# Grouped attention of one fused kernel: four key-value groups in phases, and the same work as eight overlapping half-steps

## Chip, cores and metric

The kernel runs on one NeuronCore of a Trainium2 chip, as one launch. The metric is the device time of that launch in microseconds (us), lower is better; it is the median of several executions. TensorE (PE in the profile, its weight loads PEld), VectorE (DVE), ScalarE (ACT), GpSimd (POOL) and SyncE (SP, which here only issues transfers) run their own instruction queues and meet at semaphores.

## What is computed

The program is eight blocks in a row (linear attention, mixture of experts, banded attention, LoRA experts, grouped attention, quantised feed-forward, selective scan, top-4 experts) on an activation `x` of 4 x 256 tokens by 256 channels. Before each block, `x` passes a gate: `sigmoid(x)` times a factor from a bidirectional decayed scan over a side input. The change touches the third and the fifth block.

- The fifth, grouped attention, has 16 query heads of width 128 in 4 groups; each group shares one key head and one value head. Per head: `q = rope(norm(x Wq))`, `k = rope(norm(x Wk))`, where the norm takes off the mean, divides by the root of the variance and applies a weight and a bias; then `softmax(q k^T / sqrt(128) + causal)` over 256 tokens of one batch entry, times `v`, times a gate `(1 + tanh(g/2))/2`, then `Wo`, added to `x`.
- The third, banded attention, has 16 heads of width 16 that see windows of 16-token blocks and 16 global tokens.

## The kernel before, in words

Everything is float32 with channels on the 128 partitions and the 1,024 tokens along the free axis, in two halves of 512 (`half(h)`, `HALF = 512`). PSUM is eight banks of 512 columns. A float32 matmul is two instructions on PE. All orders are written out by hand, one function for each engine; a signal such as `k["g_projected"]` counts, and `wait_ge(... .at(n))` waits until it was raised `n` times. An engine runs its queue in order, so what stands behind a wait waits too.

The grouped block (`grouped_*`) takes the 4 groups one after the other (`for g in range(m.KV)`), each in three phases over all 1,024 tokens:

1. Ten projections of 128x512 (key head and four query heads, two halves each; `JOBS`, L157), copied out by DVE (L1535), squared by ACT (L1603), summed over partitions by PE with `ones` (L157), `Ln` by ACT (L1610), then `Exp` on five blocks of 1,024 columns (L1613). Loads of ACT's function table (ACT_TABLE_LOAD) stand where `Ln` and `Exp` change places.
2. Gate and value projections with tanh (L1618) and copies (L1620), beside the rotation of the ten blocks: DVE scales and applies weight and bias (L1543, L1545), PE multiplies by a rotation matrix `g_rot`, POOL multiplies by the cosine (L1646), DVE by the sine and adds (L1551, L1553).
3. A loop over 16 units (a batch entry and a head): two score matmuls (L1703, L1704), masked maximum on DVE (L1577, L1580), exponential with row sums on ACT (L1633), reciprocal and normalisation on DVE (L1560, L1563), three transposes on PE (L1695), their copy by ACT (L1628), the product with `v` (L1713 to L1715), and the gate (L1570). Then the output projection `g_wo` for all tokens (L157) and the sum into `x` (L1590).

Beside this, `step(background, 1)` puts single instructions of the scans for blocks seven and eight (`wkv_vector`, `wkv_scalar`; L176 to L238) into the queues of DVE and ACT. In the banded block a loop over 16 groups of windows does masked scores (L1212, L1215), softmax on DVE and ACT (L1051 to L1062, L1114), transposes (L1203), their copy (L1110) and the product with values (L1231); DVE spreads the projected queries into block form (`banded_blocks`, L1012) straight from PSUM, and bank 3 is lent in turn to projections of queries and keys for later groups.

## Time and profile before

| | us |
|---|---|
| median of 3 runs | 2183.93 (2183.38 to 2186.18) |
| the profiled execution | 2181.16 |
| its span | 2179.9 |
| grouped block, from its first transfer to its last sum into `x` | 926.0 to 1443.3 |
| loop over groups in the banded block | 474.4 to 609.9 |

The profile is of one execution: its time is 2.8 us below the median of the runs, and its span 1.3 us below its time. The span is the time from the first to the last record. The busy share of an engine is an average over eight blocks with different limits, so the grouped and the banded block are read by themselves. "PEclk" is the granted TensorE clock as a share of full speed: 1.00 is 2.4 GHz and 0.50 is 1.2 GHz.

### The profile page before, as it was taken

Reading aid. Unit: us, or ns where it says so; the run is one execution under the profiler, and the core shown is the slowest. Engines: PE = TensorE matmul, PEld = TensorE weight load, DVE = VectorE, ACT = ScalarE, POOL = GpSimd, SP = SyncE. Lnnn points to the kernel's source line nnn. Section 1 sums busy time; section 2 is a strip of 40 time slices with the busy share of each in tenths; the row PEclk is TensorE's granted clock in tenths of the full one; section 3 lists DMA queues with packets and bytes.
Section 4 is the critical chain, followed back from the end, with each engine's and each line's share of the span. In section 5 each row is a group of like instructions: output and inputs, shape, how many; then the busy total and the mean of one; then the engine's idle time right before and its main releaser. Section 6 shows DMA issues by size and latency. Waiting matters only on the chain.

```text
span 2179.9 us, 17492 instructions
## 1 busy us (share of the span) xinstructions
PE 1703.0 (78%) x5814; PEld 948.5 (44%) x5814; DVE 1348.0 (62%) x2300; ACT 800.9 (37%) x1445; POOL 387.1 (18%) x261
## 2 busy tenths in 40 slices
PE   0699888877879999977887978764567777659999
PEld 0265444445643434335445453542222332226777
DVE  8474456454425636459486675876576898944565
ACT  4312434243322212243343453432354363313453
POOL 5000033110000101011020200100013765502332
PEclk9965899976759999998989989876577999969999
DMA  2000266150030000010000001000100000020110
GB/s 80 0 1 1 75 247 229 61 116 20 1 118 0 0 0 0 0 56 12 10 25 11 24 1 49 1 1 1 41 0 0 0 1 0 0 63 29 54 50 28
DMA packets 35839, 76.73 MB, mean 35 GB/s; under 512 B 5442, under 2 KB 22804, under 8 KB 33190
## 3 DMA queue, kind: packets, MB, share of 16 engines
q1 hardware_dynamic: 30662, 49.92, 7.3%
q0 software_dynamic: 5088, 25.69, 3.4%
q8 instruction: 47, 0.77, 0.2%
q14 instruction: 42, 0.34, 0.1%
HBM read 67.34 MB, written 7.21 MB: 34 GB/s over the span
## 4 chain that ended last, share of the span: by engine, by line
PE 56%; DVE 25%; issue 8%; ACT 6%; POOL 2%; PEldq 1%; DMA 1%; PEld 0%; SPq 0%; POOLq 0%; DVEq 0%; ACTq 0%
PE bank L157 41%; PE bank L2254 2%; PE bank L532 2%; PE bank L546 2%; PE bank L1215 2%; DVE g_q L1553 2%; PEldq L145 1%; DVE s_bu L2066 1%; POOL s_bu L2170 1%; DVE s_bu L2058 1%; DVE g_p L1577 1%; PE bank L1442 1%; DVE g_rs L1551 1%; DVE g_q L1543 1%; DVE g_p L1563 1%
## 5 line engine op out<-in xcount | busy, mean ns | idle before, releaser
L2170 POOL TENSOR_TENSOR s_bu<-s_rep,s_du 128x1024 f32<-128x1024 f32 x64 | 151.4, 2369 | 355.6 <-DVE s_du L2050 242.2
L2058 DVE TENSOR_TENSOR_SCAN s_bu<-bank,s_bu 128x1024 f32<-128x1024 f32 x64 | 145.8, 2279 | 22.9 <-ACT bank L2132 12.2
L2254 PE MATMUL bank<-s_bu,ident 128*128 128x512 f32 x256 | 133.6, 649 | 1.0 <-DVE s_dl L2007 0.3
L157 PE MATMUL bank<-e_xs,e_wsp 128*128 128x512 f32 x528 | 128.1, 391 | 0.0
L1646 POOL TENSOR_TENSOR g_q<-g_rs,g_rc 128x512 f32<-128x512 f32 x40 | 52.2, 1305 | 426.7 <-DVE g_rs L1545 426.7
L2132 ACT ACTIVATE bank<-s_dl,s_an 128x510 f32<-128x510 f32 x128 | 83.0, 682 | 106.1 <-DVE s_bu L2058 106.0
L157 PE MATMUL bank<-r_am,r_b 128*128 128x512 f32 x240 | 109.7, 597 | 0.0
L157 PEld LDWEIGHTS bank<-e_xs,e_wsp 128*128 128x128 f32 x528 | 99.1, 188 | 21.8 <-ACT e_cf L2444 0.7
L157 PE MATMUL bank<-conditioned,g_wqk 128*128 128x512 f32 x160 | 84.0, 656 | 21.6 <-DVE g_wqk L1530 21.6
L1406 POOL TENSOR_TENSOR r_ys<-r_y,r_y 128x512 f32<-128x512 f32 x14 | 22.8, 1631 | 433.7 <-DVE r_y L1351 433.7
L1633 ACT ACTIVATE g_p<-g_p,g_st 128x128 f32<-128x128 f32 (+1 forms) x128 | 57.2, 447 | 97.3 <-DVE g_st L1580 97.3
L2399 DVE TENSOR_TENSOR e_s<-e_s,bank 128x512 f32<-128x512 f32 (+1 forms) x50 | 34.3, 687 | 86.1 <-ACT e_s L2461 86.1
L2190 PE MATMUL bank<-s_bc,s_pick 96*128 96x512 bf16 x128 | 41.8, 411 | 56.4 <-DVE s_bu L2066 55.0
L2066 DVE TENSOR_TENSOR s_bu<-s_bu,bank 128x1024 f32<-128x1024 f32 x64 | 76.5, 1195 | 4.2 <-PE bank L2190 4.2
L157 PE MATMUL bank<-e_h,e_wdsp 128*128 128x512 f32 x264 | 75.6, 422 | 0.8 <-DVE e_h L2394 0.8
L157 PE MATMUL bank<-m_wgu,m_xs 128*128 128x512 f32 x120 | 61.9, 664 | 16.9 <-issue 15.5
L2254 PEld LDWEIGHTS bank<-s_bu,ident 128*128 128x128 f32 x256 | 52.5, 207 | 49.1 <-issue 40.9
L2461 ACT ACTIVATE e_s<-bank 128x512 f32<-128x512 f32 (+1 forms) x50 | 30.0, 599 | 116.1 <-PE bank L157 116.1
L157 PEld LDWEIGHTS bank<-r_am,r_b 128*128 128x128 f32 x240 | 46.3, 193 | 59.0 <-issue 59.0
L1603 ACT ACTIVATE g_sq<-g_q 128x512 f32<-128x512 f32 x40 | 25.2, 629 | 126.7 <-DVE g_q L1535 126.7
L1346 DVE TENSOR_TENSOR r_sl<-r_sl,bank 128x512 f32<-128x512 f32 x28 | 19.0, 678 | 82.8 <-ACT r_sl L1393 82.8
L1393 ACT ACTIVATE r_sl<-bank 128x512 f32<-128x512 f32 x28 | 16.7, 597 | 137.2 <-PE bank L157 134.1
(458 smaller groups left out, 3981.1 us busy)
## 6 DMA issues: line engine op xcount, KB each, us to landing
e_wgu<-in_e_gu SPq DMA_DIRECT2D x22, 256.0 KB, 2.7
b_vw<-b_values SPq DMA_DIRECT2D x48, 64.0 KB, 3.1
e_wd<-in_e_down SPq DMA_DIRECT2D x22, 128.0 KB, 2.6
r_w<-in_r_w SPq DMA_DIRECT2D x3, 896.0 KB, 7.9
...
```

What stands on the lines that cost most here:

```text
L157: last = e.matmul(out, lhs, rhs, start=start and n == 0, stop=stop and n == len(pairs) - 1, skip_group_check=True)
L532: last = e.matmul(banks[2 * (n % m.NPR) + i][:, cols], m.k4[j:j + 16, t, keys], m.q4[j:j + 16, t, b * T + part * P:(b + 1) * T], start=par ...
L546: last = e.matmul(bank[j:j + 32, cols], m.v[:, 2 * b + part, 32 * h:32 * h + 32], m.sm[2 * (o % m.NPR) + i][:, src], start=part == 0, stop ...
L1215: last = e.matmul(banks[n % 2][:, tile(at, m.KEYS)], m.qb[hh][:, 8 * g + w, :], m.kw[hh][:, 8 * g + w, :], start=False, stop=True, skip_gr ...
L1553: e.tensor_tensor(o, o, r, ALU.add).then_inc(k["g_q_ready"].up(), 1)
L1633: e.activation(s[:, cols], s[:, cols], ACT.Exp, bias=m.st[:, 0, c + i:c + i + 1], scale=m.SC, accum_out=m.st[:, 1, c + i:c + i + 1]).then_ ...
L1646: e.tensor_tensor(both(o), both(r), table(m.rc), ALU.mult).then_inc(k["g_cos"].up(), 1)
L2058: e.tensor_tensor_scan(b, flat(k.pairs[n % 2][:, :, :]), b, 0.0, ALU.mult, ALU.add).then_inc(k["s_scanned"].up(), 1)
L2066: e.tensor_tensor(b, b, flat(k.pairs[2][:, :, :]), ALU.mult).then_inc(k["s_weighted"].up(), 1)
L2132: e.activation(banks[2 * (n % 2) + i][:, :].rearrange("p (b t) -> p b t", t=T)[:, :, 1:T], m.dl[:, et, half(h)].rearrange("p (b t) -> p b ...
L2170: e.tensor_tensor(m.bu[n % m.NBU][:, :, :], m.rep[:, 2 * np:2 * np + 2, :], m.du[:, et, half(h)].unsqueeze(1).to_broadcast([P, 2, HALF]), ...
L2254: summed = e.matmul(banks[6][:, :], k.ident[:, :], m.bu[(n - 1) % m.NBU][:, i, :], start=np == 0 and i == 0, stop=np == m.NP - 1 and i == ...
```

## The change

In the grouped block the unit of work becomes a step `f`: one group on one half of the tokens, eight steps in all (`STEPS`). Ten passes run over eight slots each (`UNITS`); in a pass, `new` projects step n, `now` does scores and softmax for step n-1, and `old` finishes step n-2. Five projections share banks 0 and 1 with four gate projections (`grouped_free`), the sums have bank 2, scores banks 3 and 4, transposes bank 5, mixing bank 6; bank 7 holds first the values and then the two output projections. The transposes of four heads go into one bank and are copied and mixed at once (48 matmuls of 512 columns for 64 times three of 128). The rotation matrix goes: POOL multiplies by the cosine and, for half of the partitions, by the sine; DVE does the other half and the sum. Weight and bias move from DVE to ACT (`grouped_affine`); ACT first copies each variance out of the bank and takes `Ln` and `Exp` in two calls for each step. Grouped buffers now lie over those of the next block's weights, whose transfers move to the end of the block. The scans take two background steps in each slot of the first six passes. In the banded block, ACT copies the queries of the later groups to SBUF and POOL spreads them (12 of 16 calls); the projections into bank 3 move to earlier turns.

```diff
-def banded_blocks(k, e, n, bank):
+def banded_blocks(k, e, n, queries, done):
...
     own = m.heads[:, :].unsqueeze(1).unsqueeze(3).to_broadcast([P, 8, 8, m.Q])
-    e.wait_ge(*k["b_q"].at(n // 4 + 1))
-    e.tensor_tensor(m.qb[hh][:, 8 * g:8 * g + 8, :].rearrange("p w (h q) -> p w h q", q=m.Q), src, own, ALU.mult).then_inc(k["b_blocks"].up(), 1)
+    e.tensor_tensor(m.qb[hh][:, 8 * g:8 * g + 8, :].rearrange("p w (h q) -> p w h q", q=m.Q), src, own, ALU.mult).then_inc(done.up(), 1)
 
 
...
-        for at, first, bank in ((0, 4, 6), (4, 8, 3), (8, 12, 3)):
-            if at <= n < at + 2:
-                for i in range(2):
-                    banded_blocks(k, e, first + 2 * (n - at) + i, banks[bank])
...
+def banded_queries(k, e, n, bank):
+
+    m = k.banded
+    e.wait_ge(*k["b_q"].at(n + 1))
+    if n > 1:
+        e.wait_ge(*k["b_blocks"].at(4 * n - 4))
+    e.copy(m.qs[:, :], bank[:, :]).then_inc(k["b_queries"].up(), 1)
 
...
             banded_keys(k, e, 1, banks[7])
...
+        if n in (2, 6):
+            banded_queries(k, e, 2 + n // 6, banks[3])
+        if n in (4, 8):
+            banded_keys(k, e, 2 + n // 8, banks[3])
 
...
 
 
 def banded_tensor(k, e):
...
-        if n == 3:
+        if n == 2:
             project(1, 0, m.wq, banks[3], k["b_q"])
+        if n == 4:
+            e.wait_ge(*k["b_queries"].at(2))
+            project(1, 0, m.wk, banks[3], k["b_k"])
         if n == 6:
-            e.wait_ge(*k["b_blocks"].at(12))
-            project(1, 0, m.wk, banks[3], k["b_k"])
-        if n == 7:
             e.wait_ge(*k["b_keys"].at(9))
             project(1, 1, m.wq, banks[3], k["b_q"])
-        if n == 10:
-            e.wait_ge(*k["b_blocks"].at(16))
+        if n == 8:
+            e.wait_ge(*k["b_queries"].at(3))
             project(1, 1, m.wk, banks[3], k["b_k"])
...
-    NP = 5
-    JOBS = [(hd, h) for hd in [4, 0, 1, 2, 3] for h in range(NH)]
-    UNITS = [(b, hd) for b in range(NB) for hd in range(4)]
+    STEPS = 4 * NH
...
+def grouped_pieces(m, n):
...
+def grouped_rope(k, e, f, j):
+    m, n = k.grouped, 5 * f + j
+    turn, o = m.turn[n % 2], m.q[f % 2][:, j, :]
+    e.wait_ge(*k["g_affine"].at(n + 1))
+    e.tensor_tensor(both(turn[0:64, :]), both(m.rs[64:P, j, :]), table(m.rsn[64:P, :]), ALU.mult).then_inc(k.v_steps.sem, 1)
+    e.wait_ge(k.v_steps.sem, k.v_tick())
+    e.wait_ge(*k["g_cos"].at(n + 1))
+    e.wait_ge(*k["g_sin"].at(n + 1))
+    e.tensor_tensor(o, o, turn[:, :], ALU.add).then_inc(k["g_roped"].up(), 1)
...
+def grouped_gate(k, e, a, b, t):
+    m = k.grouped
+    th = m.th[a % 2][:, :, b * T + t * P:b * T + (t + 1) * P]
+    e.wait_ge(*k["g_mixed"].at(6 * a + 3 * b + (3 if t else 1)))
+    e.wait_ge(*k["g_tanh"].at(4 * a + 4))
+    e.scalar_tensor_tensor(th, th, 1.0, k.banks[6][:, :].rearrange("p (h q) -> p h q", h=m.R), ALU.add, ALU.mult).then_inc(k["g_gated"].up(), 1)
...
+    for n in range(m.PASSES):
+        new, now, old = grouped_pieces(m, n)
+        for s in range(m.UNITS):
+            if now is not None:
+                grouped_greatest(k, e, now, s)
+            if s and now is not None:
+                grouped_normal(k, e, now, s - 1)
+            if s == 0 and old is not None:
+                grouped_normal(k, e, old, m.UNITS - 1)
+                grouped_gate(k, e, old, 0, 1)
+            if now is not None and s in (0, 1, 2):
+                grouped_rope(k, e, now, 2 + s)
+            if now is not None and s == 0:
+                grouped_scale(k, e, now, 4)
+            if s in (2, 4) and old is not None:
+                grouped_gate(k, e, old, 1, s // 2 - 1)
+            if s == 6 and now is not None:
+                grouped_gate(k, e, now, 0, 0)
+            if s in (6, 7) and old is not None:
+                if n == m.PASSES - 1 and s == 6:
+                    run_out(background)
+                    arrive(k, e)
+                grouped_add(k, e, old, s - 6)
+            if new is not None:
+                if s < 5:
+                    grouped_copy(k, e, new, s)
+                if s == 5:
+                    grouped_scale(k, e, new, 0)
+                    grouped_scale(k, e, new, 1)
+                if s == 6:
+                    grouped_scale(k, e, new, 2)
+                    grouped_rope(k, e, new, 0)
+                if s == 7:
+                    grouped_rope(k, e, new, 1)
+                    grouped_scale(k, e, new, 3)
+                    if n % 2 and n // 2 + 1 < m.KV:
+                        grouped_centre(k, e, n // 2 + 1)
+                step(background, 2)
+
+
...
+def grouped_root(k, e, f, first, last):
+    m = k.grouped
+    rs = m.rs[:, first:last, :]
+    e.wait_ge(*k["g_variance"].at(5 * f + last))
+    e.activation(rs, rs, ACT.Ln).then_inc(k.a_steps.sem, 1)
+    e.wait_ge(k.a_steps.sem, k.a_tick())
+    e.activation(rs, rs, ACT.Exp, scale=-0.5).then_inc(k["g_root"].up(), 1)
...
+def grouped_tanh(k, e, f, i):
+    m = k.grouped
+    e.wait_ge(*k["g_gate"].at(4 * f + i + 1))
+    if f >= 2:
+        e.wait_ge(*k["g_down"].at(2 * f - 2))
+    e.activation(m.th[f % 2][:, i, :], k.banks[(9 * f + 5 + i) % 2][:, :], ACT.Tanh, scale=0.5).then_inc(k["g_tanh"].up(), 1)
...
+def grouped_values(k, e, f):
+    m = k.grouped
+    e.wait_ge(*k["g_value"].at(f + 1))
+    if f >= 2:
+        e.wait_ge(*k["g_mixed"].at(6 * f - 6))
+    e.copy(m.v[f % 2][:, :], k.banks[7][:, :]).then_inc(k["g_values_out"].up(), 1)
...
+    for n in range(m.PASSES):
+        new, now, old = grouped_pieces(m, n)
+        for s in range(m.UNITS):
+            turn = grouped_turn(s, new, now, old)
+            if turn is not None:
+                grouped_turned_out(k, e, *turn)
+            if new is not None and s == 7:
+                grouped_tanh(k, e, new, 0)
+            if now is not None:
+                grouped_exp(k, e, now, s)
+            if now is not None and s == 0:
+                grouped_tanh(k, e, now, 2)
+                grouped_affine(k, e, now, 4)
+                grouped_tanh(k, e, now, 3)
+            if new is not None:
+                if 1 <= s <= 5:
+                    grouped_square(k, e, new, s - 1)
+                if 2 <= s <= 6:
+                    grouped_variance(k, e, new, s - 2)
+                if s == 4:
+                    grouped_root(k, e, new, 0, 3)
+                if s == 5:
+                    grouped_values(k, e, new)
+                    grouped_affine(k, e, new, 0)
+                    grouped_affine(k, e, new, 1)
+                if s == 6:
+                    grouped_affine(k, e, new, 2)
+                    grouped_root(k, e, new, 3, 5)
+                if s == 7:
+                    grouped_tanh(k, e, new, 1)
+                    grouped_affine(k, e, new, 3)
+                step(background, 2)
     run_out(background)
+
...
+    e.wait_ge(*k["load_g"].at(48))
+    for f in range(m.STEPS):
+        for j in range(m.R + 1):
+            n, r = 5 * f + j, m.rs[:, j, :]
+            e.wait_ge(*k["g_affine"].at(n + 1))
+            if n:
+                e.wait_ge(*k["g_sin"].at(n))
+            e.tensor_tensor(both(m.q[f % 2][:, j, :]), both(r), table(m.rc[:, :]), ALU.mult).then_inc(k["g_cos"].up(), 1)
+            if n >= 2:
+                e.wait_ge(*k["g_roped"].at(n - 1))
...
+def grouped_free(k, e, f, i):
...
+def grouped_output(k, e, l, c):
+    m = k.grouped
+    e.wait_ge(*k["g_gated"].at(4 * l + 4))
+    e.wait_ge(*k["load_g_wo"].at(16 * (l // 2 + 1)))
+    if c:
+        e.wait_ge(*k["g_added"].at(2 * l + 1))
+    else:
+        e.wait_ge(*k["g_values_out"].at(min(l + 3, m.STEPS)))
+        if l:
+            e.wait_ge(*k["g_added"].at(2 * l))
+    mm(e, k.banks[7][:, :], [(m.wo[:, hd, tile(c)], m.th[l % 2][:, hd, :]) for hd in range(m.R)]).then_inc(k["g_down"].up(), 1)
...
+    for n in range(m.PASSES):
+        new, now, old = grouped_pieces(m, n)
+        for s in range(m.UNITS):
+            turn = grouped_turn(s, new, now, old)
+            if now is not None:
+                grouped_scores(k, e, now, s)
+            if turn is not None:
+                grouped_transpose(k, e, *turn)
+            if new is not None:
+                if s < 5:
+                    grouped_project(k, e, new, s)
+                if s == 4:
+                    grouped_project_values(k, e, new)
+            if s in (5, 6) and old is not None:
+                grouped_output(k, e, old, s - 5)
+            if new is not None and s > 5:
+                grouped_project_gate(k, e, new, 2 * s - 12)
+                grouped_project_gate(k, e, new, 2 * s - 11)
+            if turn is not None:
+                grouped_mix(k, e, *turn)
+            if new is not None and 1 <= s <= 5:
+                grouped_sums(k, e, new, s - 1)
```

The order of the queues, at three places. First PE in the middle of the grouped block. Names: `ident` with `g_p` are transposes, `g_pt` with `g_v` is the mixing, `g_th` with `g_wo` the output projection. Before, the end of a loop and what follows it:

```order
L1715 MATMUL bank<-g_pt_216,g_v 128x128
L1713 MATMUL bank<-g_pt_217,g_v 128x128
L1714 MATMUL bank<-g_pt_217,g_v 128x128
L1715 MATMUL bank<-g_pt_217,g_v 128x128
L157 MATMUL bank<-g_th,g_wo 128x512 x16
L157 MATMUL bank<-conditioned,g_wqk 128x512 x4
```

Now, the end of slot 4 and slot 5 of a pass:

```order
L157 MATMUL bank<-conditioned,g_wqk 128x512 x2
L157 MATMUL bank<-g_wgv,conditioned 128x128 x8
L157 MATMUL bank<-g_sq_200,ones 128x512
L1852 MATMUL bank<-g_q_209 128x128
L1853 MATMUL bank<-g_q_209 128x256
L1862 MATMUL bank<-ident,g_p_216 128x128
L1862 MATMUL bank<-ident,g_p_217 128x128
L1862 MATMUL bank<-ident,g_p_218 128x128
L1862 MATMUL bank<-ident,g_p_219 128x128
L157 MATMUL bank<-g_th_210,g_wo 128x512 x4
L1872 MATMUL bank<-g_pt_224,g_v_213 128x512
L157 MATMUL bank<-g_sq_199,ones 128x512
```

The output projection, 16 matmuls in one piece before, is now two pieces of 4 in each pass, and the first stands behind the values' projection, whose bank it takes over.

Second ACT at the same place, slots 4 and 5 (L1697 is `Ln`, L1699 `Exp`, L1739 the copy of the values, L1723 the copy of the transposes):

```order
L1697 ACT_TABLE_LOAD
L1697 ACTIVATE g_rs<-g_rs 128x1536
L1699 ACT_TABLE_LOAD
L1699 ACTIVATE g_rs<-g_rs 128x1536
L1723 COPY g_pt_224<-bank 128x512
L1714 ACTIVATE g_p_221,g_st<-g_p_221,g_st 128x128
L1714 ACTIVATE g_p_221,g_st<-g_p_221,g_st 128x256
L1682 ACTIVATE g_sq_200<-g_q_209 128x512
L1690 ACTIVATE g_rs<-bank,eps 128x512
L1739 COPY g_v_213<-bank 128x512
L1706 ACTIVATE g_rs<-g_rs,vecs 128x512 x2
```

The two table loads, once for each group before, now come twice in each step, and the copy of the values stands behind them. In the whole program ACT has 24 table loads more.

Third PE in the banded loop, turns 2 to 4. Before, and then now:

```order
L1203 MATMUL bank<-ident,b_s_155 128x128 x4
L1212 MATMUL bank<-b_msk,b_hot 128x512
L1215 MATMUL bank<-b_kw_151,b_qb_149 128x64 x8
L1231 MATMUL bank<-b_pt_159,b_vw 128x128 x8
L157 MATMUL bank<-b_xn,b_wq 128x512 x2
L1203 MATMUL bank<-ident,b_s_156 128x128 x4
```

```order
L157 MATMUL bank<-b_xn,b_wq 128x512 x2
L1217 MATMUL bank<-ident,b_s_155 128x128 x4
L1226 MATMUL bank<-b_msk,b_hot 128x512
L1229 MATMUL bank<-b_kw_151,b_qb_149 128x64 x8
L1245 MATMUL bank<-b_pt_159,b_vw 128x128 x8
L1217 MATMUL bank<-ident,b_s_156 128x128 x4
```

The projection of the queries for groups 8 to 11 went one turn up, ahead of the first transposes.

## Rows read from the trace of the kernel before

**Rows 1.** The page: busy time of the engines, share of the span, instructions

```profile
PE 1703.0 (78%) x5814; PEld 948.5 (44%) x5814; DVE 1348.0 (62%) x2300; ACT 800.9 (37%) x1445; POOL 387.1 (18%) x261
```

**Rows 2.** Windows: the grouped block (length, busy PE, PEld, DVE, ACT, POOL, clock, DMA)

```profile
925.00:1445.00 520.00, 422.72 (x1539) 248.34 (x1537) 355.26 (x905) 216.85 (x517) 52.20 (x40) 0.90 0.06 20
```

**Rows 3.** Groups by line in 925 to 1440 (busy, mean ns, idle before, releaser)

```profile
L157 PE MATMUL bank<-g_rs,g_rot 128*128 128x512 f32 x80 | 45.1, 648 | 20.9 <-DVE g_rs L1545 20.9
L1545 DVE TENSOR_SCALAR g_rs<-g_q,vecs 128x512 f32<-128x512 f32 x40 | 25.2, 629 | 1.5
L201 DVE TENSOR_TENSOR wkv_db<-wkv_db,wkv_euk 128x1024 f32<-128x1024 f32 x4 | 4.9, 1224 | 0.0
```

**Rows 4.** Timeline, phase 1 of the first group (start, us, instruction)

```profile
952.72 1.88 PE L157 MATMUL bank<-conditioned,g_wqk 128*128 128x512 f32 x4
954.43 1.02 PE L157 MATMUL bank<-g_sq,ones 128*128 128x512 f32 x2
954.63 0.69 DVE L1535 COPY g_q<-bank 128x512 f32<-128x512 f32 x1 [1.29 <-PE bank L157]
955.24 0.68 DVE L186 TENSOR_TENSOR_SCAN wkv_nb<-decay,ekv 128x256 f32<-128x256 f32 x1
955.29 1.88 PE L157 MATMUL bank<-conditioned,g_wqk 128*128 128x512 f32 x4
955.36 0.63 ACT L1603 ACTIVATE g_sq<-g_q 128x512 f32<-128x512 f32 x1 [1.37 <-DVE g_q L1535]
955.89 0.67 ACT L1610 ACTIVATE g_rs<-bank,eps 128x512 f32<-128x512 f32 x1
```

**Rows 5.** Timeline, one unit of the softmax loop

```profile
1419.59 0.28 DVE L1577 CUSTOM_DVE_ANT_0 g_p<-bank,g_msk 128x128 f32<-128x128 f32 x1
...
1420.21 0.39 PE L1703 MATMUL bank<-g_q 128*128 128x128 f32 x2
...
1420.34 0.16 DVE L1560 RECIPROCAL g_st<-g_st 128x2 f32<-128x2 f32 x1
...
1420.46 0.40 ACT L1633 ACTIVATE g_p<-g_p,g_st 128x128 f32<-128x128 f32 x1 [0.39 <-DVE g_st L1580]
...
1420.87 0.38 PE L1713 MATMUL bank<-g_pt,g_v 128*128 128x128 f32 x2
...
1420.99 0.41 DVE L1570 SCALAR_TENSOR_TENSOR g_th<-g_th,bank 128x256 f32<-128x256 f32 x1
...
1421.36 0.46 ACT L1628 COPY g_pt<-bank 128x384 f32<-128x384 f32 x1
```

**Rows 6.** Timeline, ACT from the last `Ln` to the five `Exp` of 1,024 columns

```profile
964.93 0.69 ACT L1610 ACTIVATE g_rs<-bank,eps 128x512 f32<-128x512 f32 x1 [0.64 <-PE bank L157]
965.63 1.28 ACT L1613 ACT_TABLE_LOAD   x1
966.93 4.84 ACT L1613 ACTIVATE g_rs<-g_rs 128x1024 f32<-128x1024 f32 x5
```

**Rows 7.** Timeline, POOL and DVE in the rotation

```profile
974.47 1.27 POOL L1646 TENSOR_TENSOR g_q<-g_rs,g_rc 128x512 f32<-128x512 f32 x1 [1.81 <-DVE g_rs L1545]
975.03 1.26 DVE L1553 TENSOR_TENSOR g_q<-g_q,g_rs 128x512 f32<-128x512 f32 x1
```

**Rows 8.** Windows, as rows 2, around the block's first matmuls

```profile
939.00:940.00 1.00, 1.00 (x2) 0.34 (x1) 0.44 (x1) 0.00 (x0) 0.00 (x0) 0.50 0.00 0
940.00:942.00 2.00, 2.00 (x6) 0.87 (x5) 1.15 (x3) 1.64 (x2) 0.00 (x0) 0.91 0.00 0
```

**Rows 9.** Timeline, PE's first matmul behind the end of a background job

```profile
1039.61 0.80 PE L1713 MATMUL bank<-g_pt,g_v 128*128 128x128 f32 x2 [4.26 <-ACT g_pt L1628]
```

**Rows 10.** Waits in 455 to 626, the banded block (total us, times, longest)

```profile
PE bank L157 <- DVE b_qb L1012: 6.6, 2, 3.3
...
PE bank L157 <- ACT b_kw L1085: 4.0, 1, 4.0
```

**Rows 11.** The page: its costliest group (busy, mean ns, idle before, releaser)

```profile
L2170 POOL TENSOR_TENSOR s_bu<-s_rep,s_du 128x1024 f32<-128x1024 f32 x64 | 151.4, 2369 | 355.6 <-DVE s_du L2050 242.2
```

401 lines of the change are left out of this document (184 added, 217 removed).

## Prediction

> **What bounds the kernel now.** I read the page first: PE is busy for 78% of the span and DVE for 62% [rows 1], so neither alone sets the time. Then the windows of the block that changes most: the grouped block takes 926.0 to 1443.3, 517.3 us, with PE busy for 423 of 520 us and DVE for 355 [rows 2]. PE's records overlap and many ran at half clock, so I count PE by its distances instead. Last I read the timeline for the distance from one instruction to the next and from one engine to the next, because the new order is a ring of waits and only such distances price it.
>
> The distances, at full clock. A projection holds PE for 1.71 us (952.72 to 954.43) and one product of 512 columns for 0.86 (954.43 to 955.29). DVE starts 1.91 after a projection starts, so 0.20 after its end; ACT's square starts 0.73 later; a 512-column op holds DVE for 0.61, and a square holds ACT for 0.53 [rows 4]. Two scores take 0.66 (1420.21 to 1420.87); by the same row a transpose is 0.11, four 0.44. Maximum and shift hold DVE for 0.75 (1419.59 to 1420.34), normalisation for 0.65 (to 1420.99). The exponential starts 0.87 after the maximum starts and holds ACT for 0.90 (1420.46 to 1421.36) [rows 5]. A table load is 1.28; 1,024 columns take 0.97 on ACT (4.84 for five), so 512 more cost about 0.43 and 1,536 columns 1.45 [rows 6].
>
> **Part 1, work removed and added in the grouped block.** The rotation matrix goes: 40 products of 0.86, 34 us of PE (its records sum to 45.1) [rows 3]. DVE loses 40 ops of 0.63, 25 us [rows 3]. ACT gains 40 affine calls of some 0.62, 25 us, and 24 table loads, 31 us. POOL goes from 40 ops of 1.27 to 80 [rows 7], for half of the partitions in the new ones; I give them the same 1.27, since the length is the same. In a steady pass PE then has 41 us (5 projections, 4 gates and the values at 1.71, 5 sums and 6 mixings at 0.86, 2 output pieces of 3.43, scores 5.3, transposes 2.6), DVE 42 and ACT 36. If nothing waited, eight passes would take some 340 us. They do wait.
>
> A rule of the Trainium skill bears on the loads. The trace shows one load ahead of the five `Exp` [rows 6] after one ahead of `Ln`, so two for each change there and back. The page "ScalarE: Activation LUTs" (Table sets: the hidden batching unit) says that one set holds both `ln` and `exp`, so that the pair needs one load. By it the sum below would be about 16 loads, 20 us, shorter. The queue as built has two, and I count two.
>
> **Part 2, one steady pass, slot by slot.** `G` is the start of DVE's maximum. The ring of slots 1 to 4 is: scores 0.66 and 0.20 to DVE, 0.87 and 0.90 for the exponential, square 0.53, variance 0.69, 0.05 to PE, sums 0.86. That is 4.8 us, where PE has 4.5 to 5.0 of work.
> - Slot 0: the first projection waits for a bank that ACT's third tanh frees, behind the exponential: 0.86 + 0.87 + 0.90 + 0.6 + 0.05 + 1.71 = 5.0.
> - Slot 1: DVE is last. Its slot 0 holds maximum, normalisation, gate, rotation (1.33), scale and copy, and two background steps (0.77 each on average: in the 24 steps of a job 16 scans of 0.6 [rows 4], some six ops of 1.2 [rows 3] and two shorter ones), 6.1 us. Behind them come two POOL ops. A DVE op with two SBUF inputs that starts while POOL multiplies ends 0.55 after it: 1.26 us instead of 0.68 [rows 7]. Two such waits add 2.5. So `G` is at 9.5, and the slot ends 3.3 later at 12.8: 7.8 us.
> - Slot 2: the mixing waits for the gate, behind DVE's rotation: 6.8. Slots 3 and 4: 4.8 and 4.9.
> - Slot 5: ACT issues the square root behind slot 4's variance: 0.70 + 1.30 + 1.48 + 1.30 + 1.50 = 6.3 us. Behind it stand the copy of the transposes, exponential, square, variance (0.5 + 0.9 + 0.5 + 0.6), then the copy of the values. PE's output projection needs the bank of the values. From the start of the variance, ACT has copied them after 6.3 + 2.5 + 0.6 = 9.4 us; PE begins slot 5 at 1.8, has 1.1 of scores and transposes, and then waits 6.5. Then come 3.43 + 0.86 + 0.86: 12.8.
> - Slot 6: scores and transposes 1.1; the second output piece waits 2.5 for DVE (maximum, normalisation, gate, add); then 3.43, two gates 3.42 and mixing 0.86: 11.3. Slot 7: the third gate waits for the first tanh, behind ACT's second square root (4.7): 6.8.
>
> The sum is 60.2 us, against 64.7 for half a group now (517.3 / 8).
>
> **Part 3, the block.** The first matmul comes at 8.1 instead of 9.8 us, the weights' transfer being first in SP's queue. Pass 0 has new work only: five turns of 1.71 + 0.86 and the values to ACT's variance at 14.3, then in a row square root 6.1, square to second affine 3.0, third affine 1.3, second root 4.7, tanh 0.6 and two gates 3.4: 33.5. Pass 1 has no `old`, so that slots 5 and 6 are 8.0 and 5.4, slot 7 with ACT behind it 8.7, and the centring 1.3: 52.5 with the first five slots at 29. Passes 2 to 5: 4 x 60.2, and 4 us twice for the centring of weights behind DVE's slot 7: 249. Passes 6 and 7 without background: 113. In pass 8, without projections, DVE's rotation and the two output pieces leave 33.5; pass 9 is three rounds of transposes, copy and mixing at 2.1, a gate, and two output pieces of 3.43 with their sums, 17. Each of four background jobs ends in two `Ln`/`Exp` calls of ACT with two loads; such an end cost PE 4.26 us before [rows 9] and stands in the ring again: 17. Together 8.1 + 515.5 = 524 us, +6 against 517.3.
>
> To this comes the clock. At the block's first matmuls, after 9.9 us without work, the granted share was 0.50 (1.2 GHz) up to 940 and then rose [rows 8]: four dense microseconds did two us of work. In rows 9 PE came back slow after 4.3 us without work too. Slot 5's gap of 6.5 us comes in six passes, slot 6's of 2.5 and slot 1's of 3 as well. I take 2 us for the first and 1 for each of the others, 4 x 6, and 11 for the thin first and last passes: 35 us. Its ends are 10 (only the long gaps) and 55 (each gap costs 2). The Trainium skill states the direction in "TensorE: Matmul & The Clock Gate" (Part 1): throttled is the default and activity releases it. Grouped block: +41.
>
> **Part 4, the banded block.** PE waits 6.6 us for DVE's spread queries and 4.0 for the copied keys [rows 10]; the earlier turns take both away, 10.6. The four projections also move under the normalisation that PE waits for anyway, about 1.8 us each, 7. Against it: 12 POOL ops of 2.37 or more [rows 11], during which DVE's one two-input op of each turn (L1062) waits up to 2.4; I take 5 in all. Together -13, with ends -22 (no contention, a warmer clock) and 0 (every turn held).
>
> **Small edits.** Mixing four heads at once has the same columns and fewer instructions: nothing, hidden in PE's gaps. `Ln` from SBUF after a separate variance copy is in the ring above. The later transfer of the next block's weights starts behind pass 7, some 50 us before its first reader: nothing; if that cover went, it would be one transfer of some 7 us.
>
> Sum: +41 - 13 = +28. The profiled execution would go from 2181.2 to 2209; the median stands 2.8 higher, so 2183.9 + 28 = **2212 us**.
>
> **The rivals.**
> - *PE does not wait for the values in slot 5* (faster). If ACT reached the copy as early as PE its bank, 6.5 us x 6 = 39 and the cold start behind it, 2 x 6 = 12, go: 2212 - 51 = 2161. It decides in that one wait of PE: the change gains once it is under some 3 us. For it: ACT is the least busy of the three, at 36 us in a pass, and my ring may stack waits that in truth overlap. Against it: ACT's queue order is fixed and the two loads are measured. 0.22.
> - *The clock stays up.* The gaps are mostly shorter than the 4.3 and 9.9 us that brought the low clock here, and my 35 us fall away: 2177, with 2168 to 2190 around it. 0.16, half of it faster, half the same.
> - *GpSimd and DVE collide on the path.* I charge 2.5 us in a pass. If each POOL op held DVE in full, 80 x 1.27 = 102 us, some 40 more would reach the ring: 2252. For it: scans, scale, rotation and sum all read two SBUF inputs. Against it: POOL works mostly in slots 5 to 7, where DVE has slack. 0.12.
> - That the change doesn't do what it says is excluded by the order of the queues.
>
> **How the numbers follow.** My case has 0.50, and spans 2190 to 2235 by its clock term. A measurement of this kernel can tell about 0.2%, 4.4 us, from no change. Faster: 0.22 + 0.08 = 0.30. The same: 0.08. Slower: 0.50 + 0.12 = 0.62. The range goes from 2150 (the first rival and the banded block at its better end) to 2250 (the collision's own value); some tenth lies outside on each side.
>
> **What would show it.** PE idle before the first output projection, released by ACT's L1739, 5 to 8 us in each of six passes; passes of 62 to 68 us; a granted clock in the block below the 0.90 of now; DVE's two-input ops lengthened beside POOL; no wait of PE for b_qb or b_kw. Passes under 60 us, or no wait of PE at L1739, make it wrong.

## The result and the profile after

The changed kernel takes **2208.12 us** (median of 4 runs, 2207.24 to 2209.95) against 2183.65 for the kernel before on the same chip: 1.0111 times, 95% interval 1.0093 to 1.0128. It is 24.5 us slower, and the prediction was 2212. Its profiled execution has a span of 2206.0 us. Two executions (3013.6 us of the kernel before, 2651.1 of the one with the roots without loads) ran at a granted clock of 0.62 to 0.63 and are left out of all times and intervals below.

The page of the changed kernel, the line that answers to [rows 1], and the two groups of matmuls of the grouped block in front of which PE waits most (busy us, mean ns, idle before and what ended it):

```profile
PE 1672.5 (76%) x5446; PEld 901.1 (41%) x5446; DVE 1326.0 (60%) x2216; ACT 875.4 (40%) x1484; POOL 471.5 (21%) x313
...
L157 PE MATMUL bank<-g_th,g_wo 128*128 128x512 f32 x128 | 77.3, 760 | 57.7 <-ACT g_v L1739 38.9
L157 PE MATMUL bank<-conditioned,g_wqk 128*128 128x512 f32 x160 | 86.7, 670 | 36.5 <-ACT g_th L1731 29.0
```

PE and DVE have less work than before, ACT and POOL more. What grew is PE's idle time, the number behind each bar. The waits of PE in 900 to 1500 (engine, what waits, what it waits for: total us, times, longest):

```profile
PE bank L157 <- ACT g_th L1731: 45.9, 15, 7.7
PE bank L157 <- ACT g_v L1739: 38.9, 6, 7.5
PE bank L157 <- DVE residual L1626: 18.0, 8, 2.4
```

Six waits of some 6.5 us for the copied values (6.2 to 7.5) and eight of up to 2.4 for the add of the first output piece stand there, the two that the prediction's slots 5 and 6 named. The 15 waits for a tanh (L1731) are those of its slots 0 and 7: 2.5 to 7.7 us in slot 0, 1.3 in slot 7 of passes 2 to 7. The window over the whole block, as in [rows 2]:

```profile
911.00:1488.00 577.00, 403.12 (x1197) 208.06 (x1196) 356.87 (x886) 294.14 (x572) 113.19 (x80) 0.87 0.05 18
```

The granted clock is 0.87 against 0.90. The block runs from its first transfer at 911.1 to the end of its last add at 1470.8, 559.7 us against 517.3: +42.4. The banded part in front of it became shorter: from the start of its loop to its output projections it took 135.5 us (474.4 to 609.9), now 123.0 (473.6 to 596.6), 12.5 less. That its loop also starts 0.8 us earlier need not be the change's: in the 13 traces of this case the loop starts at 470 to 481 us, behind work that no edit touches. So the length of a block tells more than its place. PE's waits in the banded part, in 470 to 640, no longer hold the two lines of [rows 10]; the longest in total is:

```profile
PE bank L1217 <- DVE b_s L1063: 17.9, 10, 2.4
```

Now the timeline of one steady pass of the grouped block, slots 5 and 6 (start us, us, instruction, idle before and its releaser):

```profile
1110.94 0.67 ACT L1690 ACTIVATE g_rs<-bank,eps 128x512 f32<-128x512 f32 x1
...
1111.63 1.28 ACT L1697 ACT_TABLE_LOAD   x1
...
1112.81 0.39 PE L1852 MATMUL bank<-g_q 128*128 128x128 f32 x2
1112.92 1.48 ACT L1697 ACTIVATE g_rs<-g_rs 128x1536 f32<-128x1536 f32 x1
...
1114.42 1.28 ACT L1699 ACT_TABLE_LOAD   x1
...
1115.72 1.48 ACT L1699 ACTIVATE g_rs<-g_rs 128x1536 f32<-128x1536 f32 x1
...
1119.55 0.57 ACT L1739 COPY g_v<-bank 128x512 f32<-128x512 f32 x1
...
1120.38 5.25 PE L157 MATMUL bank<-g_th,g_wo 128*128 128x512 f32 x8 [6.31 <-ACT g_v L1739]
...
1127.18 0.38 PE L1852 MATMUL bank<-g_q 128*128 128x128 f32 x2
...
1130.05 0.69 DVE L1626 SCALAR_TENSOR_TENSOR residual<-bank,residual 128x512 f32<-128x512 f32 x1
...
1130.88 3.67 PE L157 MATMUL bank<-g_th,g_wo 128*128 128x512 f32 x8 [2.45 <-DVE residual L1626]
```

From the start of ACT's variance to the end of the copied values it is 9.2 us (1110.94 to 1120.1); 9.4 was predicted. Both table loads of the root are there. PE starts slot 5 at 1112.81, is out of work after 1.3 us and waits 6.31. The first output piece then takes 5.25 us where the second, behind a shorter wait, takes 3.67. The granted clock (the number behind POOL's) says why: 0.69 in the first, 1.00 in the second.

```profile
1120.38:1125.46 5.08, 5.08 (x8) 2.24 (x9) 0.00 (x0) 1.17 (x2) 4.11 (x4) 0.69 0.00 0
1130.88:1134.39 3.51, 3.51 (x9) 1.60 (x10) 3.44 (x5) 3.00 (x3) 1.99 (x2) 1.00 0.00 0
```

The distance from one unit's scores (L1852) to the next gives the length of each slot. Measured, in us, for the seven passes that have both a `now` and a `new` step, passes 1 to 7 (pass 1 has no `old` one); the last row is the prediction's, without its clock term:

| pass | 0 | 1 | 2 | 3 | 4 | 5 | 6 | 7 | sum |
|---|---|---|---|---|---|---|---|---|---|
| 1 | 7.0 | 6.4 | 7.4 | 5.6 | 6.7 | 9.8 | 5.5 | 13.4 | 61.9 |
| 2 | 5.1 | 9.0 | 6.8 | 4.9 | 5.0 | 14.7 | 13.2 | 6.9 | 65.6 |
| 3 | 8.7 | 5.6 | 6.6 | 4.9 | 5.0 | 14.4 | 11.5 | 6.9 | 63.6 |
| 4 | 10.0 | 6.1 | 9.4 | 5.1 | 6.7 | 15.8 | 13.1 | 6.9 | 73.0 |
| 5 | 6.4 | 7.0 | 6.7 | 4.9 | 5.0 | 14.7 | 13.1 | 6.9 | 64.8 |
| 6 | 12.0 | 5.6 | 6.3 | 4.9 | 5.0 | 14.5 | 13.0 | 6.9 | 68.4 |
| 7 | 6.4 | 5.0 | 6.3 | 4.9 | 5.0 | 14.2 | 11.5 | 6.9 | 60.2 |
| predicted, steady | 5.0 | 7.8 | 6.8 | 4.8 | 4.9 | 12.8 | 11.3 | 6.8 | 60.2 |

### The profile page after: what moved, and what is told of

Its sections match the earlier page's. It is cut to its first block, busy times and chain, and to the rows that moved or that the text cites. A ratio compares the mean times of both kernels' runs of the same rounds, so it can differ in the third digit from the quotient of the medians.

```text
span 2206.0 us, 16987 instructions
## 1 busy us (share of the span) xinstructions
PE 1672.5 (76%) x5446; PEld 901.1 (41%) x5446; DVE 1326.0 (60%) x2216; ACT 875.4 (40%) x1484; POOL 471.5 (21%) x313
## 4 chain that ended last, share of the span: by engine, by line
PE 57%; DVE 20%; ACT 11%; issue 7%; POOL 2%; DMA 1%; PEldq 1%; PEld 0%; POOLq 0%; DVEq 0%; SPq 0%; ACTq 0%
PE bank L157 40%; PE bank L2445 2%; PE bank L532 2%; PE bank L546 2%; PE bank L1229 2%; POOL s_bu L2361 1%; PE bank L1872 1%; DVE s_bu L2257 1%; PE bank L1456 1%; DVE s_bu L2249 1%; ACT g_p L1714 1%; PEldq L145 1%; DVE g_p L1599 1%; PE bank L563 1%; PE bank L1853 1%
## 5 line engine op out<-in xcount | busy, mean ns | idle before, releaser
L1599 DVE CUSTOM_DVE_ANT_0 g_p<-bank,g_msk 128x128 f32<-128x128 f32 (+1 forms) x128 | 40.5, 354 | 149.3 <-PE bank L1853 149.2
L157 PE MATMUL bank<-g_th,g_wo 128*128 128x512 f32 x128 | 77.3, 760 | 57.7 <-ACT g_v L1739 38.9
L1723 ACT COPY g_pt<-bank 128x512 f32<-128x512 f32 x48 | 27.9, 582 | 147.1 <-PE bank L1862 147.0
L157 PE MATMUL bank<-conditioned,g_wgv 128*128 128x512 f32 x128 | 62.2, 631 | 16.9 <-ACT g_th L1731 16.9
L157 PE MATMUL bank<-m_wgu,m_xs 128*128 128x512 f32 x120 | 61.9, 664 | 16.9 <-issue 15.5
L2663 POOL TENSOR_TENSOR e_wsp<-e_wgu,e_wsp 128x512 fp32r<-128x512 f32 x22 | 33.4, 1520 | 182.8 <-ACT e_wsp L2609 182.8
```

Of the source, the lines that this page charges most:

```text
L157: last = e.matmul(out, lhs, rhs, start=start and n == 0, stop=stop and n == len(pairs) - 1, skip_group_check=True)
L1599: e.tensor_tensor_reduce(s[:, cols], k.banks[3 + n % 2][:, cols], m.msk[:, cols], 1.0, -BIG, ALU.add, ALU.max, m.st[:, 0, c + i:c + i + 1] ...
```

## The experiments

All times below are medians; "to before" is the distance to the kernel before in the same series (2182.3, 2181.2 or 2181.8 us), which for the changed kernel was +24.5. The interval is that of the ratio to the kernel before. The difference of two such distances is uncertain by some 5 to 8 us, as their two intervals together say. "Block" is the length of the grouped block in the one trace of each kernel, from its first transfer to its last add; it was 517.3 before and 559.7 in the changed kernel. It leaves out what varies ahead of the block, and so is the finer measure of an edit there, but of one execution.

| kernel | us | to before | ratio, 95% interval | block |
|---|---|---|---|---|
| banded part alone | 2171.0 | -11.3 | 0.9935 to 0.9967 | 517.4 |
| changed kernel, values first | 2203.7 | +21.3 | 1.0071 to 1.0116 | 552.8 |
| changed kernel, roots without loads | 2196.2 | +13.9 | 1.0043 to 1.0085 | 548.3 |
| changed kernel, POOL's products cut | 2193.8 | +11.5 | 1.0038 to 1.0103 | 545.7 |
| changed kernel, PE filled, 8 gaps | 2203.3 | +22.0 | 1.0070 to 1.0130 | 557.9 |
| changed kernel, PE filled, 6 gaps | 2195.0 | +13.2 | 1.0047 to 1.0091 | 545.9 |
| changed kernel, add first | 2181.6 | +0.4 | 0.9995 to 1.0026 | 534.6 |
| values first and add first | 2160.9 | -20.3 | 0.9880 to 0.9927 | 514.4 |
| and tanh first, steps dealt by slot | 2160.9 | -20.3 | 0.9884 to 0.9939 | 510.8 |
| values and add first, 12 steps a pass | 2151.1 | -30.7 | 0.9851 to 0.9881 | 503.7 |
| and tanh first | 2143.8 | -38.0 | 0.9813 to 0.9839 | 496.3 |

### The banded part alone

The kernel before, with the change's edits from the class `Banded` down to the banded part's tensor code and nothing of the grouped block.

> The kernel before with the banded part of the change alone. Theory (the turns placed earlier take PE's two waits for the spread queries and the copied keys away, 10.6 us, hide 7 of the projections and give back 5): -13, so about 2171 us, with ends at -22 and 0. Rival (the banded part gives nothing, since GpSimd's spreading is slower than DVE's, and the whole +24.5 comes from the grouped part): 2184 us.

Measured 2171.0, 11.3 below the kernel before, by the ratio 7 to 14 below. The theory holds and the rival falls; the grouped block is as long as before, 517.4 us. PE's waits in 470 to 640 show the same line, 17.9 us in ten waits, as in the changed kernel, and neither of the two.

So the slowdown of 24.5 is the sum of a gain of some 11 in the banded part and a loss in the grouped block, of about 36 us by these runs and of 42.4 by its length in the one trace.

### The values ahead of the first root

```diff
                 if s == 4:
+                    grouped_values(k, e, new)
                     grouped_root(k, e, new, 0, 3)
                 if s == 5:
-                    grouped_values(k, e, new)
```

> The changed kernel, ACT's copy of the values put ahead of the first square root instead of behind it. Theory (PE's 6.5 us before the first output piece hang on that copy alone; behind it the mixing and the sum wait for ACT's copy of the transposes and square, which still stand behind the root): PE's wait for L1739 goes, a shorter one comes before the mixing and the sum, so that 4.8 of the 6.5 us go in each of six passes, 29, and some 6 to 12 of cold restarts: about 2170 us. Rival (all of it goes, 6.5 x 6 = 39 and 12): 2157. Rival (the root's delay gives it back elsewhere in the ring): 2200 to 2208.

Measured 2203.7, and +21.3 instead of +24.5, which these runs cannot tell from no gain; the block is 6.9 us shorter. The first rival falls, and so does my forecast of 2170: this is the case in which the time is given back. The timeline of this kernel, the same pass:

```profile
1119.42 0.59 ACT L1739 COPY g_v<-bank 128x512 f32<-128x512 f32 x1 [0.53 <-PE bank L157]
...
1120.08 0.38 PE L1852 MATMUL bank<-g_q 128*128 128x128 f32 x2
...
1121.17 3.60 PE L157 MATMUL bank<-g_th,g_wo 128*128 128x512 f32 x8
...
1129.54 0.64 PE L1852 MATMUL bank<-g_q 128*128 128x128 f32 x2
```

Slot 5 is 9.5 us (1120.08 to 1129.54) instead of 14.4, as the theory said: 4.9 gained. But slot 6 is now 15.7 instead of 11.5. Over passes 2 to 7 slot 5 gives 31 us and slot 6 takes 21 of them back. Half of the 21 is the wait for the add (the change had 18.0, longest 2.4):

```profile
PE bank L157 <- DVE residual L1626: 28.4, 8, 4.2
```

The timeline of slot 6 shows what lengthened it. First the changed kernel, then this one:

```profile
1128.71 0.17 DVE L1602 TENSOR_SCALAR g_st<-g_st 128x2 f32<-128x2 f32 x1
...
1128.98 0.55 DVE L1612 TENSOR_SCALAR g_p<-g_p,g_st 128x128 f32<-128x128 f32 x2
```

```profile
1131.67 1.26 POOL L1790 TENSOR_TENSOR g_q<-g_rs,g_rc 128x512 f32<-128x512 f32 x1
1131.74 1.21 DVE L1602 TENSOR_SCALAR g_st<-g_st 128x2 f32<-128x2 f32 x1
...
1133.05 1.63 DVE L1612 TENSOR_SCALAR g_p<-g_p,g_st 128x128 f32<-128x128 f32 x2
1133.07 1.26 POOL L1794 TENSOR_TENSOR g_turn<-g_rs,g_rsn 64x512 f32<-64x512 f32 x1
...
1136.02 5.12 PE L157 MATMUL bank<-g_th,g_wo 128*128 128x512 f32 x8 [4.14 <-DVE residual L1626]
```

DVE adds the first output piece behind the maximum, shift and normalisation of slot 6. PE is now early, so that slot 6 falls beside POOL's products, which in the changed kernel were over before it: in all six passes the shift takes 0.9 to 1.2 us instead of 0.17 and the normalisation 1.6 instead of 0.55, and the add comes that much later. Behind the longer wait the second output piece is slow in all six passes (5.1 to 6.5 us, against four of six), and in four of six the scores ahead of it run at a granted 0.50. It is not ACT that DVE waits for in slot 6: the exponential that the normalisation needs ended 2.2 to 3.0 us before the slot began. The step that I had missed: the second output piece needs DVE, and how long DVE takes to the add depends on what POOL does at that time.

### The square roots without table loads

```diff
-    e.activation(rs, rs, ACT.Ln).then_inc(k.a_steps.sem, 1)
+    e.activation(rs, rs, ACT.Square).then_inc(k.a_steps.sem, 1)
```

> The changed kernel with the logarithm in the grouped block's square roots replaced by a square, which needs no table load; what is computed there is no longer the inverse root, every instruction keeps its size. 32 loads of 1.28 us go, 41 us of ACT. Theory (both roots of a pass stand in the ring, the first in front of the values in slot 5, the second in front of the tanh in slot 7): -2.6 in slot 5 and up to -2.6 in slot 7 in each of eight passes, -30 to -41, and a little of the clock, so 2165 to 2178 us. Rival (only the first root counts, the second is covered by PE's output piece and gates): 6 x 2.6 = 16 to 20, 2188 to 2192. Rival (ACT is not what the ring hangs on): above 2200.

Measured 2196.2, +13.9 instead of +24.5: 10.6 us for 32 loads of 1.28, that is 41 us of ACT. Nearest to the first rival, though under its 16 to 20. The trace is of an execution at 2206.6, 10 us above the median, but it is late ahead of the block already, which starts at 920.8 instead of 911.1; the block itself is 11.4 shorter. The wait of PE for the values fell by 2.6 each time, from 38.9 for six to:

```profile
PE bank L157 <- ACT g_v L1739: 23.6, 6, 4.9
```

Slot 7 stayed at 6.9 in passes 2 to 7, so there the second root's loads cost nothing. The third gate waits for a tanh that stands behind the copy of the transposes, and that copy waits for PE's transposes of the same slot, not for the root. The trace of the changed kernel agrees: the root is over 1.8 to 3.4 us before the slot begins, and ACT idles 3.0 to 4.7 us ahead of that copy:

```profile
1135.86 1.06 ACT L1699 ACTIVATE g_rs<-g_rs 128x1024 f32<-128x1024 f32 x1
...
1139.97 0.58 ACT L1723 COPY g_pt<-bank 128x512 f32<-128x512 f32 x1 [3.05 <-PE bank L1862]
```

My account of slot 7 had the right length for the wrong reason. Only in pass 1, whose slot 6 is short, does slot 7 hang on the root: it fell from 13.4 to 9.3. The slot lengths also tell where the rest went: slot 5 is 12.3 us shorter over passes 2 to 7 and pass 1 is 4.2 shorter; slots 0 and 1 of pass 2, behind DVE's centring of the next weights, are 2.9 longer (17.0 against 14.1), and slot 6, slow in five passes instead of four, 1.9.

### GpSimd's products cut to 8 columns

```diff
+            w = T if n < 2 else 4
-            e.tensor_tensor(both(m.q[f % 2][:, j, :]), both(r), table(m.rc[:, :]), ALU.mult)...
+            e.tensor_tensor(both(m.q[f % 2][:, j, :])[:, :, 0:w], both(r)[:, :, 0:w], table(m.rc[:, :])[:, :, 0:w], ALU.mult)...
```

and the same for the sine product: 76 of the 80 products of the block, not 78 as the text below has it, since both products of the first two heads stay whole.

> The changed kernel with GpSimd's products of the rotation (78 of its 80 ops in the grouped block) cut to 8 columns each; the rotation is then left incomplete. It prices all that GpSimd does to DVE and to the ring. Theory (two held DVE ops in a steady pass, 2.5 us, and the length of the products themselves in the rotation's chain hidden): -15 to -25, 2183 to 2193 us. Rival (GpSimd and DVE collide on the path in full): -40 or more, 2168 or less. Rival (DVE has slack everywhere): above 2203.

Measured 2193.8, +11.5 instead of +24.5: 13 us by the medians and 9 by the ratios, with runs from 2189.5 to 2203.1; the block is 14.0 shorter. That is just under the 15 to 25 of the theory; the full collision falls. The edit takes away both the holding of DVE and the length of the products themselves, and the run does not separate the two. The seven passes of the table sum to 444.8 instead of 457.5, 12.7 less, most of it (11.4) in slots 0 and 1. The groups of DVE, first of the changed kernel, then of this one (busy, mean ns, idle before):

```profile
L186 DVE TENSOR_TENSOR_SCAN wkv_db<-decay,ek 128x256 f32<-128x256 f32 x16 | 16.5, 1030 | 0.0
...
L1602 DVE TENSOR_SCALAR g_st<-g_st 128x2 f32<-128x2 f32 x64 | 14.3, 224 | 2.2
```

```profile
L186 DVE TENSOR_TENSOR_SCAN wkv_db<-decay,ek 128x256 f32<-128x256 f32 x16 | 11.9, 745 | 0.0
...
L1602 DVE TENSOR_SCALAR g_st<-g_st 128x2 f32<-128x2 f32 x64 | 10.9, 170 | 2.2
```

Without POOL's products beside it a scan is back from 1,030 ns to 745, and even the two-column shift from 224 to 170.

### PE filled while it waits for the values

```diff
+        for _ in range(6):
+            e.matmul(k.banks[6][:, :], k.ones[:, :], m.th[l % 2][:, 0, :], start=True, stop=True, skip_group_check=True)
         e.wait_ge(*k["g_values_out"].at(min(l + 3, m.STEPS)))
```

> The changed kernel with six products of 512 columns (5.2 us at full clock, written to a bank that the next mixing overwrites) put into PE's wait before each step's first output piece. Nothing else moves. In the changed kernel's trace the piece behind the 6.3 us wait takes 5.25 us, the same eight products at full clock 3.6. Theory (the gap without work brings the low clock, which lengthens the first piece by 1.65 in six passes and slot 6 by 1.6 in four): -10 to -16, so 2192 to 2198 us, and first pieces of 3.6. Rival (the low clock does not hang on this gap): 2208, pieces of 5.2 as before.

Measured 2203.3, +22.0, against a forecast of 2192 to 2198. Slot 5 came down from 14.5 to 12.6 us in five of six passes, as the theory wanted. But the edit puts the products into all eight steps, and in passes 8 and 9 PE has no such wait: the two last passes took 70 us instead of 59. The test was cut too wide, so it was made again with `range(6 if l < 6 else 0)`:

> As e5_warm, but the six extra products stand only ahead of the six first output pieces that had the 6.3 us wait, and not in passes 8 and 9, where PE had no such wait and e5_warm therefore paid 5.2 us twice. In e5_warm slot 5 came down from 14.5 to 12.6 us in these six passes. Theory (that is the whole price of this gap's low clock, 1.9 x 6 = 11): -11 to -13 against the changed kernel, 2195 to 2198 us. Rival (the clock's saving is given back elsewhere): 2203 as in e5_warm, or more.

Measured 2195.0, +13.2: 11.3 less than the change by the medians (9 by the ratios), the predicted 11 to 13; the block is 13.8 shorter. In the timeline the same eight products start behind a wait of 0.96 and are over 3.54 us later at a granted 1.00, where they took 5.08 (1120.38 to 1125.46) at 0.69 in the changed kernel:

```profile
1112.13 5.32 PE L1883 MATMUL bank<-g_th,ones 128*128 128x512 f32 x12
1118.41 3.70 PE L157 MATMUL bank<-g_th,g_wo 128*128 128x512 f32 x8 [0.96 <-ACT g_v L1739]
1121.95 1.02 PE L1872 MATMUL bank<-g_pt,g_v 128*128 128x512 f32 x2
```

No dependence changed and no useful work was added, so this is the price of the low clock behind the gap of slot 5. By the slots it is 1.9 us in each of five passes; in pass 4, where a wait of 2.0 was left behind the fill, the piece stayed slow (granted 0.68) and 0.4 was gained. Another 3 us came in slot 6, slow now in two passes instead of four. Together that is about a third of what the grouped block loses. The Trainium skill, "TensorE: Matmul & The Clock Gate" (Part 1), states the direction: the throttled clock is the default, and activity releases it. The trace agrees: 0.69 behind a wait of 6.31, 1.00 behind the fill.

### The add of the first output piece first in slot 6, alone and with the values first

```diff
         for s in range(m.UNITS):
+            if s == 6 and old is not None and n < m.PASSES - 1:
+                grouped_add(k, e, old, 0)
             if now is not None:
                 grouped_greatest(k, e, now, s)
```

> The changed kernel, DVE's add of the first output piece put first in slot 6, ahead of the maximum, the normalisation of unit 5 (which waits for an exponential behind the square root) and the gate; ACT's order as it is. Theory (PE's 2.4 us before the second output piece hang on that order): -2.4 in seven passes, 17, and some of the low clock in slot 6: 2186 to 2192 us. Rival (the mixing behind it waits instead): above 2203.

Measured 2181.6, +0.4 instead of +24.5: 24 us (22 by the ratios), at or above the upper end of the 16 to 22 that I expected. Slot 6 is 8.8 us in all six steady passes instead of 11.5 or 13.1: the 2.4 of the wait are gone, and so is the 1.6 of slow clock, which had come in four of the six. The 2.4 were DVE's own maximum, shift, normalisation and gate behind PE's scores, not a wait for ACT: in the changed kernel the exponential that the normalisation needs ended 8.4 to 9.0 us before slot 6. With this one line moved the changed kernel is level with the kernel before, though its grouped block is still longer (534.6 against 517.3): the banded part pays for the rest.

Both edits in one kernel:

> The changed kernel with both: the values copied ahead of the first root and the add first in slot 6. With the values alone, slot 5 fell from 14.5 to 9.5 us and slot 6 rose from 11.5 or 13.1 to 15.7, because PE then waited 4.2 instead of 2.4 for the add. Theory (the two waits hand the time to each other and only the two edits together free it): slot 5 at 9.5 and slot 6 at 9, a pass 9 us shorter, six times, -54: 2154 us (2145 to 2165). Rival (the two edits only add, -4.4 and -17): 2187. Rival (a third wait takes over, as the second did): above 2195.

Measured 2160.9, -20.3, that is some 45 below the changed kernel where the two edits alone gave 3 and 24 (by the blocks 45.3, where they gave 6.9 and 25.1). The rival that they only add (2187) falls: in passes 2 to 7 slot 5 is 9.0 to 10.3 and slot 6 8.8 to 10.1, and the grouped block, 514.4 us, is for the first time shorter than the 517.3 of the kernel before. The timeline of this kernel, slots 5 and 6:

```profile
1106.02 3.60 PE L157 MATMUL bank<-g_th,g_wo 128*128 128x512 f32 x8
...
1112.86 0.67 DVE L1626 SCALAR_TENSOR_TENSOR residual<-bank,residual 128x512 f32<-128x512 f32 x1
...
1115.06 3.60 PE L157 MATMUL bank<-g_th,g_wo 128*128 128x512 f32 x8
```

Both output pieces take 3.60 and neither waits. It is not the full 54: slot 7, 6.9 in passes 2 to 7 of every kernel so far, is now 7.3 to 9.8 in five of the six. The trace shows ACT's second root reaching into it. In pass 3, the copy of the transposes follows the root's `Exp` (L1701) without a pause, the tanh follows the copy, and PE waits for the tanh:

```profile
1124.32 1.06 ACT L1701 ACTIVATE g_rs<-g_rs 128x1024 f32<-128x1024 f32 x1
...
1125.28 0.57 ACT L1725 COPY g_pt<-bank 128x512 f32<-128x512 f32 x1
...
1125.74 0.60 ACT L1733 ACTIVATE g_th<-bank 128x512 f32<-128x512 f32 x1
...
1126.49 5.37 PE L157 MATMUL bank<-conditioned,g_wgv 128*128 128x512 f32 x8 [2.44 <-ACT g_th L1733]
```

It is so in exactly the five passes with the longer slot. In these POOL's products again hold slot 6's shift (0.7 to 1.1 us) and normalisation (1.6), and the root stands behind them. No run takes the root out of this kernel, so what it costs there is not measured.

### The background work dealt out otherwise

```diff
-                step(background, 2)
+                step(background, (1, 1, 1, 3, 3, 3, 2, 2)[s])
```

in DVE's and ACT's loops, and in ACT's `grouped_tanh(k, e, new, 0)` ahead of `grouped_turned_out` in slot 7.

> The kernel of e7_both, and also ACT's first tanh ahead of the copy of the transposes in slot 7, and the background steps dealt out as 1, 1, 1, 3, 3, 3, 2, 2 over the eight slots of a pass instead of 2 in each. Theory (DVE is last in slots 0 and 1, where two scans and GpSimd's products meet, and idle in slots 3 to 5): -2.5 in each of six passes for the steps and -0.6 in each of eight for the tanh, some -18 against e7_both: 2136 us. Rival (slots 3 to 5 become as long as slots 0 and 1 become short): the same as e7_both within 5.

Measured 2160.9, the same as without, against a forecast of 2136; with runs from 2155.5 to 2168.1 it tells little. Slots 0 and 1 together fell by 2.7 us in the passes without a job's end (14.0 to 11.3, 14.1 to 11.4), and slot 7 by 0.8 a pass. But the end of a background job, two calls of ACT with two loads, now fell in front of the first root in passes 1 and 4, whose slot 5 rose from 10.4 and 10.3 to 15.4 and 15.1. So the deal of the steps was made by where the ends fall:

```diff
+def grouped_steps(n):
+    return (1, 1, 1, 2, 2, 2, 2, 1) if n else (2, 2, 2, 2, 2, 3, 3, 3)
...
-                step(background, 2)
+                step(background, grouped_steps(n)[s])
```

> The kernel of e7_both, with 12 background steps in a pass instead of 16 (1, 1, 1, 2, 2, 2, 2, 1 over the slots; 19 in the first pass), so that a background job's end on ACT (two calls with two loads, 4.7 us) always falls behind slot 3 and never behind slot 7. In e7_both's trace an end behind slot 3 makes slot 4 1.7 us longer and one behind slot 7 makes the next slot 0 3.7 and 7.7 longer (the latter with the weights' centring in front). Theory (ACT's job ends and DVE's slots 0 and 1 are what is left of the ring): -2 x 2.5 in slots 0 and 1 of four passes and -7 for the ends, some 15: 2146 us (2140 to 2153). Rival (the background work of passes 6 and 7, which had none, costs as much): 2161.

Measured 2151.1, -30.7: 10 better than with 16 steps, within the range. Slot 4 is 6.7 where an end falls behind slot 3, and no slot 0 of passes 2 to 7 is above 6.3 (12.8 before). Then, on top of it, ACT's tanh calls ahead:

> The kernel of e10_steps, with ACT's tanh calls ahead: the first in front of the copy of the transposes in slot 7, the last two in front of the exponential in slot 0. PE's waits for them are its largest in e7_both (45.7 us in 15 waits, 3.0 each). Theory (slot 7 loses the copy's 0.6, slot 0 the exponential's 0.87 and 0.9 where DVE is not last): 0.6 to 2.4 in each of eight passes, -5 to -19 against e10_steps. Rival (DVE is last in slots 0 and 1 and takes the wait over): -5 or less, the slots 0 and 1 together as before.

Measured 2143.8, -38.0, and 7 better, in the block too. In the trace the gain of passes 2 to 7 is slot 7 alone, 44 us over passes 2 to 7 instead of 52; slots 0 and 1 together are no shorter, as the rival said. PE's largest wait, for a tanh until now (43.4 in 15 waits), is now for DVE's rotation:

```profile
PE bank L1859 <- DVE g_q L1593: 24.5, 14, 3.6
PE bank L157 <- ACT g_rs L1696: 21.6, 19, 6.6
```

That is where I would look next; no run tests it. This version is 1.7% faster than the kernel before (1.6% to 1.9% by the interval) and some 62 us faster than the changed one.

## Why the prediction was right, point by point

- **The banded part, -13.** Shown: -12.5 in the trace, -11.3 in the runs (7 to 14); PE has neither of the two waits.
- **The slots of a steady pass.** Where no job ends and no centring is left over (passes 2 and 5), slots 2, 3, 4 and 7 are within 0.1 us; slots 0 and 1 together are 14.1 and 13.4 against 12.8. Slot 5 is the predicted 12.8 once the clock's 1.9 is taken off (12.6 where PE was filled). Slot 6 is 11.5 with a warm clock against 11.3. The wait for the values was 6.2 to 7.5, six times, 6.5 predicted; that for the add 2.4 against 2.5. The steady pass is the firm part of the prediction. Of the signs that it named, the long wait, the clock below 0.90 and the two waits gone came true; its passes of 62 to 68 us were 60.2 to 73.0, since job ends and centring fall unevenly.
- **The clock, 35.** Shown for the largest term: 12 predicted for slot 5, and the fill gained 11.3, of which 9.8 in slot 5 by the slots. Slot 6 lost 1.6 in four of six passes, 6 as predicted; with the add first, and so no wait, it was slow in none, and with slot 5 filled in two. Slot 1's 6 and the 11 for the thin passes no run separates.
- **Contention.** 9 to 13 us for all that POOL does, predicted 2.5 in each of six to eight passes, 15 to 20. The size was too high, and it named too few ops: not only those with two SBUF inputs are held, even the two-column shift is. I had it in slot 1 alone; with the values first it also came into slot 6, where it helped to give the time back.
- **The sum of the block, +41 against +42.4, hides errors of both signs.** By stretches, clock and job ends included where I had put them: the first pass with the start 43.4 (predicted 41.6), pass 1 61.9 (56.7), passes 2 to 5 267.0 (273.5), 6 and 7 128.6 (125), the last two 58.8 (50.5), and 11 of clock for the thin first and last passes. That the whole came so near is in part luck. The terms that were mis-sized: pass 1's slot 7 was 8.7 predicted and 13.4 measured; without the root's loads it fell by 4.1. The centring was 1.3 in pass 1 and 4 each later. Its three dependent ops hold DVE from 1011.01 to 1014.84, 3.8 us, but where it stands alone, in pass 4, slots 0 and 1 together are 16.2 against 14.1 in pass 2, so it cost 2.1: slot 0 took 4.9 more and slot 1 gave 2.8 back. In pass 6, with a job's end too, they are 17.7, against 11.4 in pass 7. The job ends were 4.26 each. In pass 3 slots 0 and 1 together are 14.3 beside 14.1 in pass 2, so an end there costs next to nothing, since DVE is last in slot 1 anyway. The start with the first pass and the last two passes came out 1.8 and 8.3 over, which is what the 11 of clock was meant for.
- **Slot 7's reason was wrong.** I put the third gate behind the second root. Without that root's loads the slot kept its 6.9, and ACT is idle before it; the slot hangs on the copy of its own transposes. That 6.8 came out is luck.
- **Rival 1, PE does not wait for the values.** It did wait, 6.2 to 7.5 each time. But the price that I gave for its absence, 51, did not hold for the edit that removes it alone: 3 us. ACT's order and DVE's stand behind each other here: with the add moved the values' order is worth 21 us (2181.6 to 2160.9), and both together gave 45.
- **Rival 2, the clock stays up,** falls to the six-gap fill. **Rival 3, the full collision,** falls to the 9 to 13 us of the cut products.
- **The table loads.** The Trainium skill, "ScalarE: Activation LUTs" (Table sets: the hidden batching unit), would have one load for `Ln` and `Exp` together; the trace shows 16 at L1697 and 16 at L1699, two for each root, and my count of two held. The measured worth of all 32 is 10.6 us, so one load per root instead of two would have been worth some 5 us here, an estimate from that run.
